# Pairs of weighed states joined on GpSimd in a scan, and the expert stages of two other layouts, in a six-layer decoder kernel

## What is computed

```python
x = ln(x + mamba(x))            # L0_attn: conv, silu, selective scan over 16 states of 1024 channels
x = ln(x + cross_attention(x, ctx))   # L0_xattn: 16 heads, 722 context rows per sequence
x = ln(x + switch_ffn(x))       # L0_ffn: top 1 of 8 experts, at most 100 tokens each
x = ln(x + retention(x))        # L1_attn: 16 heads with a decay, then a gated feed forward
x = ln(x + ternary_attention(x, ctx)) # L1_xattn: ternary weights, int8 activations
x = ln(x + top2_ffn(x))         # L1_ffn: top 2 of 8 experts, hidden 2048, exact gelu
```

## Time and profile before

| | us |
|---|---|
| median of three runs | 2812.15 |
| profiled execution | 2815.17 |
| its span, first to last instruction | 2813.2 |
| scan, first dx to last sum | 89 to 532 |
| switch stage | 1237 to 1346 |
| gather, two norms, wait for retention's weights | 1346 to 1387 |
| top-2: routing until the first up product | 2227 to 2276 |
| top-2: sixteen turns, about 30.9 each | 2276 to 2771 |
| top-2: gathers, norm, output | 2771 to 2813 |

### The profile page before, as it was taken

How to read it: one execution, slowest core, us unless ns; L and a number is a source line. 1 busy time by engine, 2 the same in 40 slices (tenths; PEclk the granted TensorE clock), 3 DMA queues, 4 the chain that set the end, 5 groups by cost and what they waited for, 6 DMA issues and landing times. The chain is left out here.

```text
span 2813.2 us, 32199 instructions
## 1 busy us (share of the span) xinstructions
PE 2477.6 (88%) x12185; PEld 1240.6 (44%) x12185; DVE 1384.8 (49%) x1950; ACT 908.4 (32%) x1850; POOL 590.7 (21%) x500
## 2 busy tenths in 40 slices
PE   7899999889999999878499899875987679999993
PEld 4344444344555555436245454443664323333331
DVE  5599989422788876621535412385444511111113
ACT  3555565204533335301122110274333112212210
POOL 0366666300000000010201100000000033433333
PEclk9899999999999999989699899997998779999997
DMA  3622222444545444137410100202000242560633
GB/s 103 209 96 87 81 76 87 109 169 151 183 139 169 162 119 159 67 90 240 140 68 0 41 0 3 92 1 90 1 1 1 105 186 90 203 266 23 266 107 113
DMA packets 99256, 301.83 MB, mean 107 GB/s; under 512 B 27468, under 2 KB 57896, under 8 KB 84892
## 3 DMA queue, kind: packets, MB, share of 16 engines
q1 hardware_dynamic: 64012, 171.55, 18.5%
...
## 5 line engine op out<-in xcount | busy, mean ns | idle before, releaser
L707 POOL TENSOR_TENSOR x_rows<-ms_state,mb_C_everywhere 128x800 f32<-128x800 f32 x128 | 245.1, 1915 | 238.3 <-DVE ms_state L680 151.0
L729 PE MATMUL psum<-mb_context,mb_key_w 128*128 128x361 f32 x768 | 270.9, 489 | 8.2 <-PEq L776 6.4
L957 PE MATMUL psum<-at_Wv,at_context 128*128 128x512 f32 (+1 forms) x576 | 266.2, 601 | 0.0
L680 DVE TENSOR_TENSOR_SCAN ms_state<-ms_decay,psum 128x800 f32<-128x800 f32 x128 | 233.0, 1820 | 27.2 <-ACT ms_decay L627 18.7
L2681 PE MATMUL psum<-tf_W,tf_x_T 128*64 128x512 f32 x1024 | 231.3, 599 | 8.9 <-DMA tf_W<-in_L_W,tt_weight_row 8.9
L2736 ACT ACTIVATE tt_hidden<-psum,tf_b 128x64 f32<-128x64 f32 x512 | 112.0, 330 | 363.8 <-PE psum L2692 363.8
L2703 PE MATMUL psum<-tf_W,tt_hidden 128*64 128x512 f32 x1024 | 226.8, 595 | 0.0
L729 PEld LDWEIGHTS psum<-mb_context,mb_key_w 128*128 128x128 f32 x768 | 139.4, 193 | 142.3 <-issue 45.2
L2626 POOL DMA_INDIRECT tf_W<-in_L_W,tt_weight_row x128 | 127.2, 993 | 229.8 <-PE psum L2681 151.7
L1058 ACT ACTIVATE at_prob<-psum,at_neg_max 100x722 f32<-100x722 f32 x128 | 110.5, 864 | 145.8 <-DVE at_neg_max L1120 145.6
L1120 DVE TENSOR_REDUCE at_neg_max<-psum 100x1 f32<-100x722 f32 x128 | 115.6, 904 | 78.2 <-PE psum L978 77.8
...
## 6 DMA issues: line engine op xcount, KB each, us to landing
...
keys_dram<-x_rows SPq DMA_DIRECT2D x128, 180.5 KB, 1.9
...
```

Source lines behind the costliest of these rows:

```text
L680: nc.vector.tensor_tensor_scan(state[:, n % RH, :], decay[:, g % RA, :, :].rearrange("p b l -> p (b l)"), drive, 0.0, ALU.mult, ALU.add).t ...
L707: nc.gpsimd.tensor_tensor(seen[:, n % RH, :], state[:, n % RH, :], cC[:, n, :], ALU.mult).then_inc(weighed, 1)
L729: last = nc.tensor.matmul(side("key", u, t == KE - 1)[:, 0:SH], lhsT=wk[:, k, e * P:(e + 1) * P], rhs=keys[:, h, k, :], start=(k == 0), st ...
L957: last = nc.tensor.matmul(bank[0:rows_of(t), :], lhsT=ctxT[:, b % 2, k, t * P:t * P + rows_of(t)], rhs=wv[:, k, h * BANK:(h + 1) * BANK], ...
```

## The change

In the scan, at states 3, 7, 9 and 11 of a tile, GpSimd adds the weighed state before (in the other slot) to the one it has just weighed, in place, and TensorE sums the pair as one; it does not sum states 2, 6, 8 and 10. The other eight are summed as before. The switch stage moves its constants, first two experts' weights and biases, and the store of x by sequences into the projection before (early, keep). gather_cols replaces gather_norm and normed_cols for retention: one pass of statistics, one factor for both norms, and retention's weights requested once all y are there; x itself is normalised later, in retain. In the top-2 stage, the scores are made with tokens as output rows, y goes by an indirect scatter to the row of its choice (give), so that plain loads bring both choices back; SP's W2 loads wait for the first x; the first W1 fetches go ahead of x on GpSimd's queue; and the closing runs in the same block: ScalarE weighs the first choice, GpSimd adds x, VectorE adds the second choice and normalises.

```diff
+            if early is not None:
+                early(sp)
+            if keep is not None:
+                for b in range(NB):
+                    sp.wait_ge(normed, b + 1)
+                    sp.dma_start(keep[b * L:(b + 1) * L, :], c.x[:, b, :]).then_inc(kept, 16)
...
+        JOIN = [3, 7, 9, 11]
+        joins = lambda t, n: t * len(JOIN) + JOIN.index(n)
+        SUMS = N_ST - len(JOIN)
+        def sums_through(t, n):
+            return t * SUMS + sum(a + 1 not in JOIN for a in range(n + 1)) if n >= 0 else sums_through(t - 1, n + N_ST)
...
             def finish(i, j):
-                dve.wait_ge(summed, i * per + j * N_ST + RH)
+                dve.wait_ge(summed, (i * 2 + j) * SUMS)
...
-                    pool.wait_ge(summed, i * per + g + 1)
+                    if (n - 1) % N_ST in JOIN and t + n:
+                        pool.wait_ge(joined, joins(t, n - 1) + 1 if n else t * len(JOIN))
+                    elif t or n >= RH:
+                        pool.wait_ge(summed, sums_through(t, n - RH))
                     nc.gpsimd.tensor_tensor(seen[:, n % RH, :], state[:, n % RH, :], cC[:, n, :], ALU.mult).then_inc(weighed, 1)
+                    if n in JOIN:
+                        pool.wait_ge(weighed, i * per + g + 1 + RH)
+                        nc.gpsimd.tensor_tensor(seen[:, n % RH, :], seen[:, n % RH, :], seen[:, 1 - n % RH, :], ALU.add).then_inc(joined, 1)
                     if last and j == 1:
...
                     if n == 0:
                         pe.wait_ge(finished, t + 1)
-                    pe.wait_ge(weighed, i * per + g + 1 + RH)
-                    add(lambda p, cols: seen[p, n % RH, cols], n == 0, n == N_ST - 1).then_inc(summed, 1)
+                    if n + 1 not in JOIN:
+                        if n in JOIN:
+                            pe.wait_ge(joined, joins(t, n) + 1)
+                        else:
+                            pe.wait_ge(weighed, i * per + g + 1 + RH)
+                        add(lambda p, cols: seen[p, n % RH, cols], n == 0, n == N_ST - 1).then_inc(summed, 1)
                     if n in GATE_AT:
...
             pe.sem_inc(side_taken, RS)
...
+    def early(sp):
+        for j in range(2):
+            for n, (w, name) in enumerate(((w1, "L0_W1"), (w2, "L0_W2"))):
+                sp.dma_start(w[j][:, :, :], dram[name][j]).then_inc(w_loaded[j][n], 16)
+        sp.dma_start(b1[:, :, :], dram["L0_b1"]).then_inc(b_loaded, 16)
+        sp.dma_start(b2[:, :, :], dram["L0_b2"].partition_broadcast(CAP)).then_inc(b_loaded, 16)
     def sync(sp):
         sp.sem_inc(w1_used, 2)
         sp.sem_inc(w2_used, 2)
-        sp.dma_start(b1[:, :, :], dram["L0_b1"]).then_inc(b_loaded, 16)
-        sp.dma_start(b2[:, :, :], dram["L0_b2"].partition_broadcast(CAP)).then_inc(b_loaded, 16)
-        with sp.Fori(0, NE // 2) as i:
+        with sp.Fori(0, NE // 2 - 1) as i:
             for j in range(2):
                 for n, (w, used, name) in enumerate(((w1, w1_used, "L0_W1"), (w2, w2_used, "L0_W2"))):
-                    sp.wait_ge(used, i * 2 + j + 1)
-                    sp.dma_start(w[j][:, :, :], dram[name][bass.ds(i * 2 + j, 1)].rearrange("a p k n -> (a p) k n")).then_inc(w_loaded[j][n], 16)
+                    sp.wait_ge(used, i * 2 + j + 3)
+                    sp.dma_start(w[j][:, :, :], dram[name][bass.ds(i * 2 + j + 2, 1)].rearrange("a p k n -> (a p) k n")).then_inc(w_loaded[j][n], 16)
     def gpsimd(pool):
         pool.sem_inc(y_free, 2)
         pool.wait_ge(table_ready, 2)
-        pool.wait_ge(x_stored, 16)
+        pool.wait_ge(x_stored, 16 * NB)
         for e in range(NE):
...
+            def early(sp):
+                for n in "qk":
+                    sp.dma_start(w[n][:, :, :], dram["L1_w" + n]).then_inc(w_loaded[n], 16)
+                for dst, src in ((bias[:, :, :], dram["L1_b_rows"].partition_broadcast(L)), (bo[:, :], dram["L1_bo"].partition_broadcast(L)),
+                                 (decay[:, :, :], dram["decay"]), (gn[:, :, :], dram["L1_gn_rows"].partition_broadcast(L))):
+                    sp.dma_start(dst, src).then_inc(rows_loaded, 16)
+                for n in "vgo":
+                    sp.dma_start(w[n][:, :, :], dram["L1_w" + n]).then_inc(w_loaded[n], 16)
+            mv, rstd = sb2("mean_var", [L, NB, 2]), sb2("x_rstd", [L, NB])
+            gather_cols(c, gate, row, y_dram, vec, w_in, early, mv, rstd)
+            retain(c, vec, x1, mv, rstd, w, w_loaded, rows, rows_loaded, [(w_in, "L1_w_in"), (b_in, "L1_b_in")])
         normed_cols(c, "re_norm2", x1, vec, 4, None)
...
+        @block.sync
+        def _(sp):
+            sp.dma_start(vec[:, :, :], dram["L1_vec"]).then_inc(vec_loaded, 16)
+            for b in range(NB):
+                sp.wait_ge(y_loaded[b], 16)
+            early(sp)
...
+        def _(pool):
+            own = Chain(pool, chain_p)
+            for b in range(NB):
+                nc.gpsimd.indirect_dma_start(y[:, b, :], None, y_dram[:, :],
+                                             bass.IndirectOffsetOnAxis(ap=row[:, 0, b:b + 1], axis=0)).then_inc(y_loaded[b], 16)
+            own(nc.gpsimd.memset(power[:, :], -0.5))
+            for z, (lo, hi) in enumerate(groups):
+                pool.wait_ge(var_ready, hi)
+                own(nc.gpsimd.tensor_scalar(both[:, lo:hi], mv[:, lo:hi, 1], 1.0 + EPS, EPS * EPS, ALU.mult, ALU.add))
+                nc.gpsimd.tensor_tensor(both[:, lo:hi], both[:, lo:hi], power[:, lo:hi], ALU.pow).then_inc(both_ready, 1)
+            own(nc.gpsimd.tensor_scalar(rstd[:, :], mv[:, :, 1], EPS, None, ALU.add))
+            own(nc.gpsimd.tensor_tensor(rstd[:, :], rstd[:, :], power[:, :], ALU.pow))
+        @block.vector
+        def _(dve):
+            own = Chain(dve, summed)
+            for z, (lo, hi) in enumerate(groups):
+                for b in range(lo, hi):
+                    dve.wait_ge(y_loaded[b], 16)
+                    own(nc.vector.scalar_tensor_tensor(c.x[:, b, :], y[:, b, :], gate[:, 0, b:b + 1], c.x[:, b, :], ALU.mult, ALU.add))
+                    own.add(nc.vector.bn_stats(stats[:, b, :], c.x[:, b, :]))
+                own.settle()
+                for b in range(lo, hi):
+                    nc.vector.bn_aggr(mv[:, b, :], stats[:, b, :]).then_inc(var_ready, 1)
+            turned.grant(dve, 1)
+            dve.wait_ge(vec_loaded, 16)
+            for z, (lo, hi) in enumerate(groups):
+                dve.wait_ge(both_ready, z + 1)
+                for b in range(lo, hi):
+                    nc.vector.tensor_scalar(xn[:, b, :], c.x[:, b, :], mv[:, b, 0:1], both[:, b:b + 1], ALU.subtract, ALU.mult).then_inc(normed, 1)
+            for b in range(1, NB, 2):
+                turned.wait_full(dve, b)
+                for k in range(KD):
+                    last = nc.vector.tensor_scalar(c.xT[:, k, b * L:(b + 1) * L], turned.bank(b)[:, k * L:(k + 1) * L], vec[:, k, 0:1],
+                                                   vec[:, k, 1:2], ALU.mult, ALU.add)
+                last.then_inc(turned.done(b), 1)
...
                 dve.wait_ge(rows_loaded, 64)
-                nc.vector.tensor_tensor(x1[:, u // 2, :], c.x[:, u // 2, :], bo[:, :], ALU.add).then_inc(x_biased, 1)
+                b = u // 2
+                nc.vector.tensor_scalar(c.x[:, b, :], c.x[:, b, :], mv[:, b, 0:1], x_rstd[:, b:b + 1], ALU.subtract, ALU.mult).then_inc(x_normed, 1)
+                dve.wait_ge(x_normed, b + 1)
+                nc.vector.tensor_tensor(x1[:, b, :], c.x[:, b, :], bo[:, :], ALU.add).then_inc(x_biased, 1)
...
+    y = free[0][0:L].rearrange("p n k f -> p (n k f)").rearrange("p (q b d) -> p q b d", q=TOP, b=NB)
+    rows = free[1][0:L].rearrange("p n k f -> p (n k f)")[:, 0:NB * D].rearrange("p (b d) -> p b d", b=NB)
+    y_loaded = [sem(f"y_loaded_{b}") for b in range(NB)]
+    weighed, added, summed, normed, sent = sem("first_weighed"), sem("first_added"), sem("vector_chain"), sem("rows_normed"), sem("sent")
+    src = y_dram.rearrange("(q b l) d -> l q b d", q=TOP, b=NB)
+    def sync(sp):
+        for j in range(2):
+            sp.wait_ge(stored[j], 16 * (NPAIR // 2))
+        for b in range(NB):
+            for q in range(TOP):
+                sp.dma_start(y[:, q, b, :], src[:, q, b, :]).then_inc(y_loaded[b], 16)
+        for b in range(NB):
+            sp.wait_ge(normed, b + 1)
+            sp.dma_start(c.out[b, :, :], c.x[:, b, :]).then_inc(sent, 16)
+        sp.wait_ge(sent, 16 * NB)
+    def scalar(act):
+        act.wait_ge(share_ready, 1)
+        for b in range(NB):
+            act.wait_ge(y_loaded[b], 16 * TOP)
+            nc.scalar.activation(y[:, 0, b, :], y[:, 0, b, :], ACT.Copy, scale=share[:, 0, b:b + 1]).then_inc(weighed, 1)
+    def gpsimd(pool):
+        for b in range(NB):
+            pool.wait_ge(weighed, b + 1)
+            nc.gpsimd.tensor_tensor(rows[:, b, :], y[:, 0, b, :], c.x[:, b, :], ALU.add).then_inc(added, 1)
+        norm.root(nc, pool)
+    def vector(dve):
+        chain = Chain(dve, summed)
```

(47 more changed lines are left out.)

274 lines of the change are left out of this document (136 added, 138 removed).

## The result

The changed kernel takes 2773.03 us (median of 4, 2762.3 to 2780.64) against 2811.82 us for the one before (median of 4): ratio 0.986, 95% interval 0.9826 to 0.9895. The forecast was 2763 us with a range of 2742 to 2785. The profiled execution took 2774.24 us with a span of 2772.4.

The account below looks back on a forecast made before the run. TensorE bounds the scan, VectorE 7% behind; elsewhere chains of DMA, routing and norms. Scan -15, switch -10.7, retention -15.1, top-2 front -2.5, close -6 sum to -49.3 us: 2765.9 profiled, 2763 median, range 2742 to 2785.

Parts of the forecast that it names:

- the third rival: Top-2 stage: its two ends give nothing, +3 and +1 us, for 2775 us in all; chance 0.10.
- the first: Scan: GpSimd's joins eat the scan's gain while the rest holds, for 2778 us in all; chance 0.18.
- The saving of TensorE: Scan: four sums fewer per tile at 0.83 us save 3.3 us, so TensorE alone would need 50.5 us.
- VectorE's floor: Scan: without its waits for ScalarE and GpSimd, VectorE takes 50.7 us a tile, a hair above TensorE.
- two or three such slips, 51.7: Scan: late scans waiting on joins, allowed for in a tile of 51.7 us, 2.1 us saved per tile.
- The hand count: Scan, states 6 to 11: waits followed make the scan of state 14 about 0.6 us late.
- VectorE over 95%: Scan: sign to look for in the new profile, VectorE busy at over 95%.
- The sign named for this: Scan: TensorE's idle time before the sums would now be put down to GpSimd; no size given.
- the gather's term: Switch: issue of x's gather to the first expert product takes 6.1 us instead of 15.2, so -9.1 us.
- both terms: Retention's start: one pass of statistics, -10.2 us, and weights loaded earlier, -4.9 us.
- Top-2 front: Top-2 start: scores +2.3, table +0.7, earlier fetches -5, Gelu some 2.5 us late; -2.5 us in all.
- Close: Top-2 end: GpSimd's adds and VectorE's sums take turns, 8 x 2.1 = 16.8 us; -6 us.

Follow-up runs that it names:

- the weights late: Changed kernel with the switch experts' first weights and biases issued at the start of the switch stage again, router's weights and x's store still early: 2772.04 us, ratio 0.9863.
- an experiment: Changed kernel with retention's weights issued in retention's own block and, in the close, both weighed sums on VectorE: 2777.47 us, ratio 0.9868.

## Why the prediction was right, and where not

**The range and the sign held**; the likeliest case, 2763, was 10 us low. The measured 2773.03 lies nearer to the third rival (2775) and the first (2778), of which the third did not happen: it had both ends of the top-2 stage at nothing.

**The scan's size was wrong, -7.1 for -15.** The saving of TensorE was sized well: per tile its busy time went from 315.8 x 54.0/320 = 53.3 us to 302.7 x 52.8/320 = 49.9, 3.4 for 3.3. VectorE's floor, a tile less its waits for ScalarE and GpSimd, is 52.8 - 17.4/6.06 = 49.9 us in 150 to 470, where 50.7 was forecast. It is lower by dx, 0.6 us shorter, which the forecast did not see; that this helped is luck. The failed term is "two or three such slips, 51.7": 1.0 us of waits a tile was allowed where 2.9 stand. The hand count went through the ring of two buffers correctly and named the place (states 6 to 11), and its slip of 0.6 us at state 14 came as 0.79. But it missed the 1.48 us at state 10: it left out that GpSimd enters that place held 1.8 us by TensorE's sum. Nor did I ask what each of the four saved sums is worth: the one of state 2, which I counted among the two that matter, is worth nothing. The first rival's sentence, under 0.3 us to spare per join around states 6 to 11, was right, and its chance of 0.18 too small.

**VectorE over 95%** did not come: it is busy for 294.58 of 320 us, 92%, and was for 91% before. TensorE's idle time before its sums in 150 to 500 us grew from 4.8 us to 13.5, but only 3.9 of it is put down to GpSimd; 9.5 is VectorE's finish of the tile before (line 676). Another 7.2 us stands before the key products, for ScalarE. The sign named for this was half right.

**Switch, -8.8 for -10.7.** From the first score product to the first expert product it is 25.6 us; 24 was forecast. The scores took 8.38 us where the one of the earlier trace rows took 6.91: the granted clock was 0.50 from 1225 to 1229, after the waits of the norm, and 0.77 in the next 4.8 us. With the weights late, at a granted clock of 1.00, they took 5.53, and in the kernel with joins 3, 7, 11, 15, also at 5.53, the stretch is 22.7. So the gather's term (9.2 measured, 9.1 forecast) is right in size, and this place differs by 3 us between executions with the clock. One reading of it was wrong: 19.6 us is not the landing of the first gather, whose rows were used 13.1 us after its issue. The sum did not use it. The last 1.1 us stand between the last y's store and the first gather, 6.08 for 4.94; their cause was not tried.

**Retention, -15.0 for -15.1**, both terms confirmed, the weights' 4.9 by an experiment, the single pass by the trace (transposes 10.4 us earlier for 10.2).

**Top-2 front, -3.1 for -2.5**: right in sum, wrong in parts. The scores took 10.83 us where 11.4 was forecast, all at a granted clock of 0.50; against the 9.1 us of scores and turning before, that is 1.7 us more, and 2.3 was forecast. The first product gained 8.8 where I had 5, and the stall at the Gelu and at the fetch behind W1 took 5.8 where I had 2.5. Both fetches stand at the end of GpSimd's queue beside SP's loads; I counted only b1's.

**Close, -6.0 for -6**: partly luck. GpSimd's first add began 9.1 us after the last y where 7.9 was forecast, and the sums came 1.91 us apart and not 2.1, so two errors of about 1.3 us cancelled. The loads ran at 246 to 256 GB/s in most slices, not 240. Over the executions of the same close the stretch from the last y to the end takes 36.2 to 38.2 us, a gain of 4 to 6.
